# A graph network kernel in 25 blocks: their closing barriers without GpSimd's drain

## The reference, cut to what matters

```
xn = layernorm(x)
x = x + attention_over_edges(xn, src, dst) + mixer0(xn)   # 53125 edges, 8 heads, softmax by dst
x = x + ffn0(layernorm(x))                                # each node goes to 1 of 8 experts, capacity 489
xn = layernorm(x)
x = x + convolution(xn[src], edge_attr, radial(edge_emb)) summed by dst + mixer1(xn)
x = x + ffn1(layernorm(x))                                # a graph attention over 32768 edges and 3125 loops
                                                          # scores 4 experts; the best 2 are mixed
return x
```

## Time and profile before

| | us |
|---|---|
| median of three runs | 3129.1 |
| lowest and highest run | 3125.21, 3131.22 |
| the profiled execution, its own time | 3132.5 |
| its span, first to last instruction | 3130.8 |

### The profile page before, as it was taken

The page is one execution under the profiler, slowest core; times in us unless marked ns, Lnnn a source line. Parts: engine busy times, 40 slices in busy tenths (PEclk is TensorE's granted clock), DMA queues, the critical chain, the costliest instruction groups (busy, mean ns, idle before and its releaser), DMA issues. The chain is left out here.

```text
span 3130.8 us, 41052 instructions
## 1 busy us (share of the span) xinstructions
PE 2334.8 (75%) x11127; PEld 1532.2 (49%) x11128; DVE 2012.6 (64%) x4054; ACT 1372.2 (44%) x3793; POOL 1760.6 (56%) x1789
## 2 busy tenths in 40 slices
PE   3996777777776666599969577777777788888781
PEld 2554555555554555166614223233336677776660
DVE  4564999999998887011063489999994632222588
ACT  0222566556543443321126488888882222222230
POOL 1544778777772045667751477777762057777100
PEclk8998888888887555799969799998998789999895
DMA  3213666666660100133221233333321121111004
GB/s 102 54 39 113 205 202 202 208 205 201 203 191 1 56 30 16 47 117 104 71 75 51 61 98 100 103 100 100 100 83 17 32 55 36 36 36 36 16 1 175
DMA packets 163880, 287.79 MB, mean 92 GB/s; under 512 B 55384, under 2 KB 99421, under 8 KB 163662
## 3 DMA queue, kind: packets, MB, share of 16 engines
q0 software_dynamic: 79568, 187.15, 21.5%
q1 hardware_dynamic: 71834, 79.09, 8.1%
q10 hardware_dynamic: 12260, 18.94, 1.7%
HBM read 248.79 MB, written 36.25 MB: 91 GB/s over the span
## 5 line engine op out<-in xcount | busy, mean ns | idle before, releaser
L2333 PE MATMUL cv_ps<-cv_msg,cv_hot 128*128 128x512 f32 x880 | 435.5, 652 | 165.1 <-DVE acc L2383 125.0
L2320 POOL DMA_INDIRECT cv_x<-x_tab,e_src x440 | 447.4, 1017 | 195.8 <-issue 94.8
L960 POOL DMA_INDIRECT at_kv<-kv_tab,e_src x440 | 464.6, 1056 | 154.8 <-issue 85.9
L2754 POOL DMA_INDIRECT gs_h<-h_tab,fc_q x312 | 294.4, 944 | 177.9 <-issue 93.6
L2333 PEld LDWEIGHTS cv_ps<-cv_msg,cv_hot 128*128 128x128 f32 x880 | 179.6, 210 | 420.7 <-ACT cv_msg L2346 216.3
L2004 POOL DMA_INDIRECT pairs<-gating_pair,gating_place x288 | 275.8, 958 | 159.3 <-issue 69.1
L2346 ACT ACTIVATE cv_msg<-cv_x,factors 128x64 f32<-128x64 f32 x1320 | 356.5, 333 | 0.0
L2383 DVE TENSOR_TENSOR acc<-acc,cv_ps 128x256 f32 x880 | 307.5, 413 | 38.1 <-PE cv_ps L2333 31.4
L2344 ACT ACTIVATE cv_msg<-cv_x,factors 128x256 f32<-128x256 f32 x440 | 217.8, 495 | 127.4 <-DMA cv_x<-x_tab,e_src 127.4
L1096 PE MATMUL at_a<-at_kv,at_hot_e 128*128 128x264 f32 x880 | 253.7, 418 | 7.3 <-DVE at_kv L1169 5.0
L1071 PE MATMUL at_q<-q_parts,at_hot_n 128*128 x1320 | 214.4, 314 | 40.2 <-DVE at_kv L1153 32.3
(11 more groups left out here) (545 smaller groups left out, 4610.8 us busy)
## 6 DMA issues: line engine op xcount, KB each, us to landing
x_w<-in_L_ffn_w SPq DMA_DIRECT2D x16, 1024.0 KB, 8.1
at_rel_row<-e_rel_rows SPq DMA_DIRECT2D x55, 256.0 KB, 4.7
experts_out<-gs_y ACTq DMA_DIRECT2D x20, 512.0 KB, 2.7
x_y<-experts_out SPq DMA_DIRECT2D x20, 512.0 KB, 4.8
at_kv<-kv_tab,e_src POOLq DMA_INDIRECT x440, 3.8
cv_x<-x_tab,e_src POOLq DMA_INDIRECT x440, 2.8
kv_tab<-p_qkv SPq DMA_DIRECT2D x25, 256.0 KB, 2.0
gs_h<-h_tab,fc_q POOLq DMA_INDIRECT x312, 2.3
```

Of the source, the lines that this page charges most:

```text
L960: nc.gpsimd.indirect_dma_start(out=kv[:, t % (RING * Q4), 0:2 * D], out_offset=None, in_=kv_tab, in_offset=bass.IndirectOffsetOnAxis(ap=e. ...
L2320: nc.gpsimd.indirect_dma_start(out=xg[:, i % RT, u, :], out_offset=None, in_=x_tab, in_offset=bass.IndirectOffsetOnAxis(ap=e.src[:, t:t + ...
L2333: nc.tensor.matmul(ps[u % R][:, :], hot[:, i % 2, u, :], msg[:, i % 2, u, :], start=True, stop=True).then_inc(summed, 1)
L2754: nc.gpsimd.indirect_dma_start(out=hg[:, i % RT, u, :], out_offset=None, in_=h_tab, in_offset=bass.IndirectOffsetOnAxis(ap=e.src[:, i * U ...
```

## The change

```
-        with nc.Block() as block:
+        with nc.Block(no_gpsimd_drain=True) as block:
```

## The result

Five runs of the changed kernel gave 3104.2 to 3113.9 us, median 3110.4; five of the kernel before beside them 3125.2 to 3131.2, median 3126.9. The medians differ by 16.5 us; the ratio on record is 0.9941 (95% interval 0.9926 to 0.9955), some 18 us faster. Timed once more, beside other runs of before, the same kernel gave 0.9960 (0.9941 to 0.9979), some 12.5 us. The forecast itself, 3114.4 on 3129.1, is a ratio of 0.9953; it lies between the two measurements and inside both intervals.

What follows compares the result with a forecast made beforehand. No engine fills the span: the kernel is a row of 25 stretches, each as long as its slowest engine. Terms -16.56 + 1.65 + 0.2 = -14.7 us take 3129.1 to 3114.4 us; own range 3111 to 3118, whole range 3109 to 3131.

Steps and rivals of the forecast that it cites:

- Three exposed drains go: At L1672, L1369 and L1415, where GpSimd arrives last: its drains of 6.016, 3.972 and 6.571 us vanish, -16.56 us.
- Twenty-two drains in the shade give nothing: At the other 22 barriers DVE, SP or ACT is late anyway, so removing GpSimd's drain gains 0.
- One more event semaphore: At the 22 barriers where GpSimd isn't last, an added semaphore costs 0.075 us each, +1.65 us; ends 0.4 and 2.2.
- Finished transfers stay on the books: GpSimd's transfers, unwalked at block ends, may be paid at L94, L96 or L3281: 0 to 15.3 us, taken as 0.2.
- Both rivals in which the walk moves: Drains at L94, L96 or L3281 walk the finished transfers at 0.082 us each; chances 0.11 and 0.09.
- the second: Rival: the walk also follows into the next execution's first drain, L3281, another 7.3 us: +7.7, 3136.8 us; chance 0.09.
- the price of the first: Rival: exposed walks of 7.3 and 8 us at the recyclings, L94 or L96: +0.4, 3129.5 us; chance 0.11.
- Dealing with them while issuing: Within L1369 or L1415, GpSimd handling finished transfers between scatters costs 0 to 1.4 us; taken as 0.
- the third rival: GpSimd's books fill in L1369 or late L1415, exposing a 6.6 us walk among scatters: -8.1, 3121 us; chance 0.08.
- The fourth: Rival: at the seams the time belongs to the transfers, not the drain; only +1.65 us remains, 3130.8 us; chance 0.04.
- 2 us for the spread of the runs: Part of the forecast's own range of 3111 to 3118 us, beside the semaphores' and L94's ends.
- the stages behind the seams only start earlier: Behind L1672, L1369 and L1415 no timer or spanning transfer was found, so all 16.56 us reach the end.

Runs made afterwards that it cites:

- the drain that I added: The full change plus one plain GpSimd drain in front of each of the two recyclings, against the kernel before: ratio 1.0000.
- the third fed kernel: New barrier at L1672, L1369, L1415 alone, 18 idle PE products ending L1415 and 14 small ones starting return0, against the kernel before: 0.9939.
- the changed kernel with the settings: The full change plus six 128x1280 memory settings at the end of GpSimd's list in L1415, against the kernel before: 0.9949.

## Why the prediction was right, and where it was not

The mechanism held at the seams and the range did not; the last part of this section names the step that failed.

*Three exposed drains go: right.* At all three lines GpSimd stayed last, as the earlier trace rows had it, and from its last branch to its release 16.6 us went, for 16.56 forecast. The stages as a whole are 17.6 and 17.9 us shorter. The excess lies inside them, where L1672 and L1415 differ by half a microsecond between two profiles of before.

*Twenty-two drains in the shade give nothing: right.* The kernel with only these removed isn't faster.

*One more event semaphore: right in kind, 0.26 us low.* The 22 barriers cost 1.91 us and not 1.65; the 0.2 that the sum held for L94, which cost nothing, makes up for it by luck. 21 of the 22 barriers take 0.05 to 0.08 us longer, 1.47 in all, so 0.070 each where 0.075 was reckoned; the interval of the earlier trace rows was the right measure and not the duration. One barrier, the L482 ahead of the first recycling, takes 0.44 longer in each profile that has the new form there: DVE's event semaphore starts 0.43 us behind its drain. I have no reason for it.

*Finished transfers stay on the books: right.* The price per transfer was as read from the earlier trace rows. The two walks took 7.26 and 8.96 us, some 88 and 109 transfers, where 7.3 and, out of 6.6 to 9.2, 8 were said. L94 drops them at no price. Both rivals in which the walk moves are refuted by L94 and L96, the second also by L3281 in the profiled execution, and the price of the first is confirmed by the drain that I added.

*Dealing with them while issuing: right at zero.* The odd gap of the earlier trace rows is no sign of it: 1.68 to 1.69 us stand at the 114th scatter of the block in all sixteen profiles, with or without 121 more transfers unwalked, so it doesn't follow the books. GpSimd's waits for its own issue in L1369 are 42 of at most 0.3 us. The one gap of over 3 us in L1415, 16.8 at its third scatter, is a wait for PE that stood there before with 17.5. No stall appeared, which refutes the third rival. The fourth, that the drain is not the cause, is refuted by the gaps that closed.

*What failed: "2 us for the spread of the runs", and that the stages behind the seams only start earlier.* The measured 3110.4 us is below the range, and the span fell by 19.1 us, more than the 18 that I had set as a limit. The sum puts the change in the length of every stage behind the seams at nothing. But return0 came out 3.1 us shorter in the first pair of profiles, with less time at 1.2 GHz: 17.6 of the three stages, less 1.9 of semaphores, and 3.1 of return0 make 18.7 of the 19.1. Whether the change caused these 3.1 us stays open. What the change does at the seams and barriers themselves, 16.6 less 1.9, is the 14.7 of the forecast. The mis-sized term is the spread. I had taken 2 us from three runs; the runs of before that lie beside the experiments go from 3120.7 to 3143.6, the two profiles of the changed kernel differ by 9.7 us, and single stages swing by 3 to 11 us over the sixteen profiles (L941 3.7, L2311 7.6, L2238 5.7, L1539 11.1). Against that a range from 3111 to 3118 was too narrow, while its middle was sound: 18.4 us in the first measurement, 12.5 in the second, 14.7 forecast.

## What to carry to other kernels

A drain on the engine that issues indirect transfers costs some 0.08 us here for each that it has not yet dealt with, though they have landed: where that engine is last at a barrier it is worth dropping, and where it isn't, the drain is free and the replacement costs 0.07 us. A barrier without it no longer says that the engine's work is done; I take it to be safe where the list ends with waits for what the others will touch, or where the others wait for it themselves. And before a change of half a per cent is judged, time the same kernel against itself: here one program's runs spread over 20 us, and five runs gave 14.7 us for a drain of 6.6.

## What the runs showed of the hardware

The granted clock stayed at 1.2 GHz for 10 to 40 us while PE worked without a break at the start of return0, and in the third fed kernel it fell to 1.2 GHz at 1577 us within such work. Why it rises when it does, no run here shows. The spread of the times goes with the clock in part: over 29 runs of before on one chip time and mean granted clock have a correlation of -0.75; the slowest three had 0.847, 0.848 and 0.851, the fastest three 0.853, 0.853 and 0.852.

In the changed kernel with the settings, DVE's two small operations on slot_i took 0.82 and 1.10 us beside them, 0.18 each without (the first in the earlier trace rows). Each ended 0.03 to 0.04 us behind the end of a setting. DVE's own memory setting, which followed while GpSimd's still ran, took its usual 5.39 us. So work that GpSimd carries past such a barrier can slow some operations of DVE in the next block. The Trainium skill's page "SBUF — State Buffer", section "SBUF: two separate sides", describes a pair of ports that GpSimd shares with those DVE operations that run in a two-port mode or, against a GpSimd operation that reads, have two inputs; whichever starts first holds the pair for its whole instruction. The two ends agree with it; in which mode these operations ran, no run here shows.
